# A macaron layer on one core: down products with tokens as weights, their sums read from the banks

## The reference

```python
x = x + 0.5 * ffn(layernorm(x), ...)
x = x + attention(layernorm(x), ...)      # 16 heads of 16, LoRA on q, k, v and o
x = x + 0.5 * ffn(layernorm(x), ...)

def ffn(x, ...):
    # product keys: top 8 of the sums of two top-8 lists choose experts among 512
    ew = silu(x @ down_embed[indices].T) * softmax(scores)
    mlp = (silu(x @ gate_w) * (x @ up_w)) @ down_w     # 256 -> 1024 -> 256
    return mlp + ew @ up_embed[indices]
```

## Time and profile before

| | |
|---|---|
| median of three runs | 1014.11 us |
| profiled execution, span | 1013.4 us |
| TensorE (PE) busy | 913.6 us, 90% |
| VectorE (DVE) busy | 710.8 us, 70% |
| ScalarE (ACT) busy | 485.9 us, 48% |
| GpSimd (POOL) busy | 231.1 us, 23% |
| feed-forward stage of layer 0, products | about 47 to 254 us |
| feed-forward stage of layer 1, products | about 802 to 1010 us |
| attention with projections | about 257 to 742 us |

### The profile page before, as it was taken

How to read it: one execution, slowest core, us unless ns; L and a number is a source line. 1 busy time by engine, 2 the same in 40 slices (tenths; PEclk the granted TensorE clock), 3 DMA queues, 4 the chain that set the end, 5 groups by cost and what they waited for, 6 DMA issues and landing times. The chain is left out here.

```text
span 1013.4 us, 15033 instructions
## 1 busy us (share of the span) xinstructions
PE 913.6 (90%) x4368; PEld 616.7 (61%) x4368; DVE 710.8 (70%) x1322; ACT 485.9 (48%) x939; POOL 231.1 (23%) x194
## 2 busy tenths in 40 slices
PE   2598989898698999999999999999975899999996
PEld 2587878786584555555555555555344778777875
DVE  4776758574767888888888888888327774757583
ACT  3533323232243366666666666666744633232322
POOL 3343434343405000000000000000005252435252
PEclk9799999999696799999999999999978898999998
DMA  7000000000005422222222222200050000000000
GB/s 255 24 12 1 0 0 0 0 1 1 6 7 95 72 37 43 44 45 44 42 42 42 43 42 42 42 2 2 0 178 1 1 1 0 21 0 21 1 21 21
DMA packets 20452, 31.69 MB, mean 31 GB/s; under 512 B 5568, under 2 KB 14784, under 8 KB 20416
## 3 DMA queue, kind: packets, MB, share of 16 engines
q1 hardware_dynamic: 20416, 31.25, 14.2%
HBM read 12.09 MB, written 2.10 MB: 14 GB/s over the span
## 5 line engine op out<-in xcount | busy, mean ns | idle before, releaser
L1187 DVE TENSOR_REDUCE maxima<-max_ps 128x1 f32<-128x512 f32 x512 | 319.5, 682 | 70.0 <-PE max_ps L1038 69.9
L1146 ACT ACTIVATE probs<-score_ps 128x512 f32<-128x512 f32 x512 | 267.4, 601 | 103.9 <-PE score_ps L1052 102.4
L1038 PE MATMUL max_ps<-k_stack,q_stack 128*128 128x512 f32 x512 | 221.8, 453 | 6.4 <-DVEq L1225 4.2
L1052 PE MATMUL score_ps<-q_stack,k_stack 128*128 128x512 f32 x512 | 203.3, 405 | 2.4 <-ACT probs L1146 2.3
L560 ACT ACTIVATE ffn_tanh<-ffn_gate_ps 128x512 f32<-128x512 f32 x96 | 57.4, 598 | 264.6 <-PE ffn_gate_ps L50 264.6
L1038 PEld LDWEIGHTS max_ps<-k_stack,q_stack 128*128 128x128 f32 x512 | 99.3, 197 | 137.5 <-DVE maxima L1187 119.1
L611 POOL TENSOR_TENSOR ffn_hidden_lo<-ffn_hidden,ffn_hidden_hi 128x512 fp32r<-128x512 f32 x96 | 123.6, 1287 | 243.9 <-ACT ffn_hidden_hi L568 243.9
L684 DVE SCALAR_TENSOR_TENSOR ffn_gated<-ffn_tanh,ffn_gate_ps 128x512 f32<-128x512 f32 x96 | 65.7, 685 | 120.5 <-ACT ffn_tanh L560 120.4
L1079 PE MATMUL mixed_ps<-probs,values 128*32 128x512 f32 x1024 | 136.4, 605 | 0.0
L1052 PEld LDWEIGHTS score_ps<-q_stack,k_stack 128*128 128x128 f32 x512 | 96.3, 190 | 30.3 <-ACT probs L1146 13.1
L505 PE MATMUL ffn_out_ps<-ffn_hidden_hi,ffn_late_hi 128*128 128x512 f32 x192 | 81.3, 424 | 1.5 <-POOL ffn_hidden_lo L611 1.5
(11 more groups left out here) (148 smaller groups left out, 1221.9 us busy)
## 6 DMA issues: line engine op xcount, KB each, us to landing
q_stack<-q_hi SPq DMA_DIRECT2D x64, 64.0 KB, 2.3
q_stack<-q_lo SPq DMA_DIRECT2D x64, 64.0 KB, 2.3
k_stack<-k_hi SPq DMA_DIRECT2D x64, 64.0 KB, 2.3
k_stack<-k_lo SPq DMA_DIRECT2D x64, 64.0 KB, 2.3
x_sb<-in_x SPq DMA_DIRECT2D x4, 512.0 KB, 6.2
ffn_gate_stage<-in_gate SPq DMA_DIRECT2D x2, 1024.0 KB, 8.4
ffn_up_stage<-in_up SPq DMA_DIRECT2D x2, 1024.0 KB, 10.4
ffn_late_stage<-in_down SPq DMA_DIRECT2D x2, 1024.0 KB, 12.0
```

Source lines behind the costliest of these rows:

```text
L1038: pe.matmul(max_ps[:, i % RING, :], q_stack[s][:, j, qt * P:(qt + 1) * P], k_stack[s][:, j, half * HALF:(half + 1) * HALF], start=True, st ...
L1052: pe.matmul(score_ps[:, i % RING, :], k_stack[s][:, j, kt * P:(kt + 1) * P], q_stack[s][:, j, half * HALF:(half + 1) * HALF], start=True, ...
L1146: act.activation(probs[:, kt % 2, j, half * HALF:(half + 1) * HALF], score_ps[:, i % RING, :], ACT.Exp, scale=SCORE_SCALE).then_inc(probs_ ...
L1187: v.reduce_max(maxima[:, par, i // 2, i % 2:i % 2 + 1], max_ps[:, i % RING, :], axis=AXIS_X).then_inc(taken, 1)
```

## The change

The down product changes its roles. The hidden values of 128 tokens are the weights, and 256 columns, a whole row of `down_w`, stream. A unit has 4 tiles of tokens and 3 matmuls of 256 columns for each, 12 instead of 6. The sums come out as tokens x columns, four tiles in two banks, so `update` reads `out_ps` itself, as soon as `down_done` says that the chunk's last down product is done. `copy_out`, `turn_out`, `out_rows` and two semaphores go. Since `out_ps` is now what `update` reads, the wait for `x_updated` goes from unit 8 to the down product of unit 0. Two tiles share a bank, so only the first matmul of the chunk in a bank has `start`.

```diff
-        out_rows = sb("out_rows", [P, KT, CHUNK], F32)
-        out_ps = psum("out_ps", [P, KT, CHUNK], F32)
+        out_ps = psum("out_ps", [P, CT, DIM], F32)
...
-        def down_weight(u, k):
-            piece, column = (u if u < FT else u - FT + 12) // 2, u % 2 * DIM + k * P
-            return late_hi[:, piece, column:column + P], late_lo[:, piece, column:column + P]
+        def down_rows(u):
+            piece, column = (u if u < FT else u - FT + 12) // 2, u % 2 * DIM
+            return late_hi[:, piece, column:column + DIM], late_lo[:, piece, column:column + DIM]
...
                 if e == 0:
                     pe.wait_ge(mixed, (c + 1) * 2 * MIX_STEPS)
-                    pe.wait_ge(x_updated, c * CT + 1)
...
             def down(c, u):
                 pe.wait_ge(hidden_lo_done, c * UNITS + u + 1 + HIDDEN_RING)
-                for k in range(KT):
-                    w_hi, w_lo = down_weight(u, k)
-                    x_hi, x_lo = hidden_hi[:, u % SPLIT_RING, :], hidden_lo[:, u % SPLIT_RING, :]
-                    pe.matmul(out_ps[:, k, :], w_hi, x_hi, start=(u == 0), stop=False)
-                    pe.matmul(out_ps[:, k, :], w_lo, x_hi, start=False, stop=False)
-                    out = pe.matmul(out_ps[:, k, :], w_hi, x_lo, start=False, stop=(u == UNITS - 1))
+                if u == 0:
+                    pe.wait_ge(x_updated, c * CT + 1)
+                w_hi, w_lo = down_rows(u)
+                for tt in range(CT):
+                    at = slice(tt * P, (tt + 1) * P)
+                    x_hi, x_lo = hidden_hi[:, u % SPLIT_RING, at], hidden_lo[:, u % SPLIT_RING, at]
+                    first, last = u == 0 and tt % 2 == 0, u == UNITS - 1 and tt % 2 == 1
+                    pe.matmul(out_ps[:, tt, :], x_hi, w_hi, start=first, stop=False)
+                    pe.matmul(out_ps[:, tt, :], x_hi, w_lo, start=False, stop=False)
+                    out = pe.matmul(out_ps[:, tt, :], x_lo, w_hi, start=False, stop=last)
                 out.then_inc(down_done, 1)
-
-            def turn_out(c):
...
             def update(c):
-                v.wait_ge(out_turned, c + 1)
+                v.wait_ge(down_done, (c + 1) * UNITS + SPLIT_RING)
                 for tt in range(CT):
                     v.scalar_tensor_tensor(out=x_sb[:, c * CT + tt, :],
-                                           in0=mix_ps[:, tt // 2, tt % 2 * DIM:(tt % 2 + 1) * DIM], scalar=0.25,
+                                           in0=out_ps[:, tt, :], scalar=0.25,
                                            in1=x_sb[:, c * CT + tt, :], op0=ALU.mult, op1=ALU.add
                                            ).then_inc(x_updated, 1)
```

More of the change, by code:

```diff
@@ L357, in ffn_block @@
         mix_turned = sem("mix_turned")
-        out_copied = sem("out_copied")
-        out_turned = sem("out_turned")
         x_updated = sem("x_updated")
@@ L501, in down @@
                 pe.wait_ge(hidden_lo_done, c * UNITS + u + 1 + HIDDEN_RING)
-                for k in range(KT):
-                    w_hi, w_lo = down_weight(u, k)
-                    x_hi, x_lo = hidden_hi[:, u % SPLIT_RING, :], hidden_lo[:, u % SPLIT_RING, :]
-                    pe.matmul(out_ps[:, k, :], w_hi, x_hi, start=(u == 0), stop=False)
-                    pe.matmul(out_ps[:, k, :], w_lo, x_hi, start=False, stop=False)
-                    out = pe.matmul(out_ps[:, k, :], w_hi, x_lo, start=False, stop=(u == UNITS - 1))
-                out.then_inc(down_done, 1)
-            def turn_out(c):
[L511 to L517, removed]
+                if u == 0:
[8 more added lines that the diff above has]
+                    out = pe.matmul(out_ps[:, tt, :], x_lo, w_hi, start=False, stop=last)
+                out.then_inc(down_done, 1)
             pe.sem_inc(down_done, SPLIT_RING)
@@ L533, in _ @@
                 unit(c + 1, DOWN_LAG)
-                turn_out(c)
             down(CHUNKS - 1, 0)
@@ L540, in _ @@
                 down(CHUNKS - 1, u)
-            turn_out(CHUNKS - 1)
         @block.scalar
@@ L569, in round_hidden @@
                                ).then_inc(hidden_hi_done, 1)
[L571 to L574, removed]
             unit(0, 0)
@@ L587, in _ @@
                 round_hidden(c + 1, 0)
-                copy_out(c)
                 unit(c + 1, 2)
@@ L594, in _ @@
             round_hidden(CHUNKS - 1, UNITS - 1)
-            copy_out(CHUNKS - 1)
         @block.gpsimd
```

## The result

The changed kernel takes 1053.81 us (median of 4 runs) against 1013.41 us (median of 4 runs of the kernel before beside it): a ratio of 1.0401, 95% interval 1.0377 to 1.0426, so 4% slower. The forecast was 1050.3 us in a range of 1038 to 1063. The profiled execution spans 1052.1 us, 38.7 more than before; the sum of the prediction, made against the span, was 1049.6. The medians lie 40.4 us apart, the spans 38.7. Where both are known, an execution takes about 2 us more than its span, so the profiled execution of the kernel before was most likely its slowest, 1015.41 us, and a difference of spans comes out 1 to 2 us small.

What follows compares the result with a forecast made beforehand. TensorE's order of work was taken as the clock of the feed-forward stages; span 1013.4 + 24.2 (moved wait) + 13.2 (clock) + 3.3 (down products) - 4.5 (stage ends) = 1049.6 us, 1050.3 as median; range 1038 to 1063.

Steps and rivals of the forecast that it cites:

- The wait that moves: At six chunk boundaries the first down product waits for VectorE's update, 4.04 us later each: +24.2 us, removed turn included.
- TensorE's clock: Behind each boundary's idle time the clock falls to its lower level, 2.2 us each: +13.2 us (9.7 to 20).
- Down products: In 78 paid units, 12 products of 256 columns replace 6 of 512: +3.3 us (-4.2 to +7.0).
- the upper bound: For a 256-column down product: the 0.014 us rest goes with each load, so it costs 0.121 us.
- the two covered down products: Those of units 4 and 5, ahead of line 496's wait; their extra time only shortens TensorE's idle time, costing nothing.
- The ends of the stages: At both stage ends update starts where ScalarE's copy did, 2.26 us earlier in the first: -4.5 us in all.
- (a): Rival: a 256-column down product costs only 0.109 us, making the down term -4.2 us: 1043 us; chance 0.08.
- (b): Rival: 256-column down products are dear, 0.21 us apart, 90 us in place of 3.3: 1137 us; chance 0.06.
- (c): Rival: TensorE's idle time at unit 8 makes up the boundary's loss, up to 17 us back: 1033 us; chance 0.04.
- (d): Rival: at the boundary update is done when TensorE comes to it, so the wait costs nothing: 1008 us; chance 0.02.

Runs made afterwards that it cites:

- the wait alone: Kernel before with one wait more: a chunk's first down product also waits for x_updated; 512-column products, copy and turn stay; 1053.19 us, ratio 1.0406.
- the halves alone: Kernel before with each 512-column down product made as two of 256; layout, copy, turn and waits stay; 1019.24 us, ratio 1.0058.
- the early update: Changed kernel with VectorE's update(c) ahead of unit(c+1, 2), the chunk's statistics left behind it; 1008.05 us, ratio 0.9951 to the kernel before.

## Why the prediction was right

Point by point, against the difference of the spans, 38.7 us:

- **The wait that moves** was forecast at +24.2. The boundary of the changed kernel has 5.03 us from the last up product to the first down product and had 1.02: 6 x 4.01 = 24.1. The kernel with the wait alone leaves 24.2. That both engines come to it only behind `unit(c+1, 2)` could be read in the code; that VectorE would end no sooner could be read in its rows.
- **TensorE's clock** was forecast at +13.2, between 9.7 and 20. The low clock with work grew from 26.6 to 55.7 us, x 0.46 = 13.4; 28.35 us of it lie behind the six boundaries. The forecast of 2.2 us a boundary met 28.35 x 0.46 / 6 = 2.2. That a fall comes at each boundary was argued from rows; its length was a choice between rows of 3.41 and 7.00 us, and the six turned out at 2.88 to 5.46, 4.7 on average. That 2.2 hit so closely is in part luck.
- **Down products** were forecast at +3.3, with -4.2 to +7.0 as bounds. This is the term that was mis-sized: the halves alone cost 6.3. It took the middle of 0.1135 and 0.121, and the spacing is 0.120: the 14 ns go with each instruction or its load, as the upper bound had it. What wasn't in the sum at all is that, as the timeline shows, the gate products behind a run of down products come a little late (0.24 and 0.23 in place of 0.227), about 0.02 us a unit. Nor does the wait of unit 8 stay as it was: it is 20.5 us in place of 22.3, as it would if the two covered down products took their extra time out of it.
- **The ends of the stages** were forecast at -4.5. From the end of the last down product to the update it was 2.30 us and is 0.04: 2 x 2.26. Right.
- Together 24.1 + 13.4 + 6.3 - 4.5 = 39.3, 0.6 above the 38.7.
- **The rivals.** (a), 0.109 us for a product, falls: it is 0.120. The Trainium skill's page "TensorE: Matmul & The Clock Gate" (Part 2, Back-to-back issue gap) gives N/2.4 + 2.5 ns, which is the same 109 ns for 256 columns; the trace doesn't agree, and the trace decides. (b), 0.21 us at the full clock, falls by the same rows; the 0.213 of the lower clock is no support for it, as a 512-column product takes 0.427 there. (c), an absorbed stall, falls: the wait of unit 8 gave 1.8 us in all, which the down products took. (d) was priced at 1008 for a kernel whose `update` is done when TensorE comes to it; the early update is that kernel, and took 1008.05. The agreement is partly luck: its down term was 3.3 and not 6.3, it started from 1014.1 where the kernel before beside that run took 1012.74, and the low clock differs too. But the point from which it decides was the right one.

## What to carry to other kernels

When a result is read from where it was summed, the bank is held until the reader has run, and the wait for that moves to the next use of the bank: look in both engines' written orders where the reader stands and where the next writer stands, before counting the copies that go. Here the reader was done 4.8 us after TensorE had come to the end of its other work, and moving it ahead by one unit turned a loss of 4% into a gain of 0.5%. Idle time of TensorE costs more than its length where the clock falls behind it. What helped most here was to put other work of the same engine in front of the wait: 21.5 us for the kernel before, 1013.19 to 991.67.

## What the runs showed of the hardware

- Splitting a product of this type isn't free in proportion: 512 columns stand 0.227 us apart, 256 columns 0.120, 128 columns 0.111. Per column that is 0.44, 0.47 and 0.87 ns. At 128 columns the loads of weights, 0.11 us apart, set the pace.
- At the lower clock the extra 14 ns, which a product has over its columns at the full clock, vanish: 512 columns take 0.427 us and 256 columns 0.213, so 1.20 columns a ns at both sizes. A low stretch therefore costs 0.44 to 0.47 of its length and not a half; three pairs of kernels bear this out (21.4 us by 0.46 and 21.0 measured; 21.6 and 21.7; 20.8 and 20.7, the last two with the shortened wait in them).
- Twenty useless products in each of the six stalls made the program 20.3 us faster than leaving TensorE idle (1053.81 to 1033.52).
- The same idle time of 2.56 us was followed by a fall of the clock at some places and by none at others. What decides is open. Behind six idle times of about 4.7 us the low clock came each time, for 2.88 to 5.46 us of work.
